# Router steps of the last attention stage on other units, and its score products in pairs

## The chip, the cores and the metric

The kernel runs on one core of a Trainium2 chip. The metric is the device time of one execution in microseconds. Instructions run on four engines: PE (TensorE), DVE (VectorE), ACT (ScalarE) and POOL (GpSimd). SP only issues DMAs, in its program order. Engines meet at semaphores, and each engine's instruction order is written out by hand.

## The reference

Two layers on x (2 batches, 512 rows, 1024 wide) and a context (2 x 1024 x 1024). The change lies where the second layer's grouped attention ends and its router begins:

```
q = (latents @ Wq.T)                    # 16 heads of 96, 4 key heads
scores = einsum('bkgqd,bksd->bkgqs', q, k) * scale      # 1536 keys
attn = softmax(scores)
out = einsum('bkgqs,bksd->bkgqd', attn, v)
x = x + tanh(g) * (out @ Wo.T)
# router and expert biases, 64 experts, the 8 best
logits = layernorm(x) @ router_weight.T + router_bias
scores = softmax(logits);  topk_w, topk_idx = top_k(scores, 8)
out = flat * w_sum + w_dense @ expert_bias
x = x + tanh(g) * out
```

Each fp32 operand of a product is split into a high and a low fp16 part, and three of the four partial products are summed.

## The kernel before, in words

Attention is done in 128 units m of 128 queries of one head against 1536 keys. They form 8 stages t of 16 units u (UPS = 16), a stage being one batch and one key head. The last stage begins at LAST = 112. Below, "unit 3" is the unit 3 of the last stage, "unit -1" the one before that stage; scores(3), exp(3) and so on are its steps. The tables of line 288 onwards count units in the same way.

In a unit, each engine does the following, in this order.

- **PE:** scores(u), six products over all 128 rows (the heads, L857) and three over 32 rows each (the rest, L835), into one of two sets of three PSUM banks. Then side work: router(i) for query tile i (24 small products, L599 with 64 columns), expert_turn(i) (L906), one half of an output product (L599 with 512 columns, nine products; wo_at gives the units 2, 3, 5, 6, 10, 11, 14 and 15) or expert_mix (L911, L912). Last weigh(u-3), 24 products that weigh the values (L880, L882), into bank 6.
- **DVE:** row_max(u) (L1659), for a router its logits (L1684) and choose_first (L1692 onwards), add_out (L1653) or add_mix (L1731), take_out(u-3) (L1673, L1675) and at last expert_stats(i) (L1398 onwards).
- **ACT:** take_o on every fourth unit, expert_weights (w_exp), exp(u) (L1325), the high cast hi(u) (L1054, region_b), expert_norm(i) (L1057 and L1054 on stage), expert_exp (L1301), expert_scale (L1057 on x_res).
- **POOL:** choose_rest(i), take_low_o, expert_low(i) (stage), the low part lo(u) (region_y, L1824), and for a tile with stats its deviations (rstd, nmr).
- **SP:** turn_o (L526), turn4(i) (L531, the transpose of tile i for the router), the transposes of hi(u) (L547) and lo(u) (L553). All DMAs of this stretch go through this one queue.

A tile's way to the router is expert_stats, deviations, expert_norm, expert_low, turn4, router; from there logits, expert_exp, choose_first, choose_rest, expert_turn, expert_weights, then two expert_mix and the store. Each step has a table from unit to tile. expert_stats(i) waits for the tile's last output product.

Four waits matter. scores(u) waits for exp(u-2), which frees its banks. weigh(u-3) waits for both transposes of unit u-3 and for take_out(u-4). router(i) and expert_turn(i) write bank 6, as weigh does: they wait for take_out(u-4), and the weigh behind a router waits until DVE has read its logits (lg_step), the one behind an expert_turn until ACT has made w_exp (wx_ok). expert_scale(i) and choose_rest(i) are waited for by add_mix and expert_turn.

Outside the last stage the rests of two units are paired: at an even unit u PE runs heads(u), rest(u), waits for exp(u-1), and runs rest(u+1) into the other banks; unit u+1 has then its heads alone. In the last stage, units are not paired.

After unit 15 comes a tail that is written out step by step: the last three weigh, the last output products, the routers of tiles 5, 6 and 7 and the last stores.

Of the kernel before, what the change touches and what calls it, by code (L numbers as in the profile page):

```python
# [54 lines left out]
def flamingo(nc, x_d, ctx_d, ctx_t_d, par_d, ident_d, wk_d, wv_d, wq_d, wo_d, wb_d, bb_d, ft_d,  # L55
             coef_d, mask_d, enc_d, rw_d, rb_d, eb_d, out_d):
    with ExitStack() as ctx:
# [227 lines left out]
        WQ_LOAD, WO_LOAD = {8: 0, 9: 1, 10: 2, 12: 3}, {3: 0, 4: 1, 5: 2, 6: 3}  # L285
        KV_LOAD = {0: 0, 1: 1, 2: 2, 7: 3, 13: 4}
        LAST = NU - UPS
        STATS4 = {-3: 0, -1: 1, 3: 2, 6: 3, 11: 4, 15: 5}
        NORM4 = {-2: 0, 0: 1, 4: 2, 7: 3, 12: 4}
        LOW4 = {-1: 0, 1: 1, 5: 2, 8: 3, 13: 4}  # L290
        ROUTE = {2: 0, 5: 1, 8: 2, 11: 3, 15: 4}
        CHOOSE = {3: 0, 6: 1, 9: 2, 12: 3}
        CHOOSE_REST = {4: 0, 7: 1, 10: 2, 13: 3}
        TURN_W = {6: 0, 9: 1, 12: 2, 14: 3}
        SCALE_X = {6: 0, 9: 1, 12: 2, 14: 3}
        MIX = {7: (0, 0), 8: (0, 1), 9: (1, 0), 12: (1, 1), 13: (2, 0)}
        STORE = {9: 0, 13: 1}

# [30 lines left out]
        def use(m, r):  # L329
            return 16 * (m // r + 1)  # L330
# [5 lines left out]
        def _(sp):  # L336
# [201 lines left out]
            for m in range(NU):  # L538
                t, u = m // UPS, m % UPS
                if o_at(m) is not None and m < NU - 1:  # L540
                    turn_o(o_at(m))
                if m - LAST in LOW4:
                    turn4(LOW4[m - LAST])
                if m >= PT:
# [50 lines left out]
        def _(pe):  # L595
# [243 lines left out]
            def scores(m):  # L839

                t, u = m // UPS, m % UPS
                b, qt, h = t % B, u // G, u % G
                if u == 0:
                    pe.wait_ge(k_ld[b], 5 * use(t, B))
                pairs = 2 <= m < LAST
                rest_behind = m % 2 == 0 or not pairs
                if m < G:
                    pe.wait_ge(q_set, min(m + 1, NJ))
                elif u == 0:
                    pe.wait_ge(q_free, 2 * NJ * (t + 1))  # L850
                    pe.wait_ge(q_dup, G * t)
                    pe.wait_ge(q_ld[b], 64 * ((t + t % 2) // 2))
                if m >= 2:
                    pe.wait_ge(e32_ok, m - 1)
                for n in range(2):
                    for sb_ in range(NSB):
                        ins = nc.tensor.matmul(bank(NSB * (m % 2) + sb_), q_head[:, b, h, n, qt * P:(qt + 1) * P],  # L857
                                               k_head[:, b, n, sb_ * 512:(sb_ + 1) * 512],
                                               start=rest_behind and n == 0, stop=not rest_behind and n == 1)
                if rest_behind:  # L860
                    ins = score_rest(m, False)
                    if pairs:
                        if m + 1 < G:
                            pe.wait_ge(q_set, min(m + 2, NJ))
                        pe.wait_ge(e32_ok, m)
                        score_rest(m + 1, True)
                ins.then_inc(sc_ready, 1)
# [59 lines left out]
            for m in range(NU):  # L927
# [4 lines left out]
                last = m - LAST  # L932
                if last in ROUTE:
                    pe.wait_ge(o_ok, m - LAG)
                    router(6, ROUTE[last])
                if last in TURN_W:
                    pe.wait_ge(o_ok, m - LAG)
                    expert_turn(6, TURN_W[last])
                w = wo_at(m)
# [16 lines left out]
                if m >= LAG:  # L956
                    if last in ROUTE:
                        pe.wait_ge(lg_step, ROUTE[last] + 1)
                    if last in TURN_W:
                        pe.wait_ge(wx_ok, TURN_W[last] + 1)  # L960
                    weigh(m - LAG)
# [90 lines left out]
        def _(act):  # L1052
# [261 lines left out]
            for m in range(NU):  # L1314
                t, u = m // UPS, m % UPS
                last = m - LAST
                if o_at(m) is not None and m < NU - 1:
                    take_o(o_at(m))
                if last in TURN_W:
                    expert_weights(6, TURN_W[last])  # L1320
                rows = ps[:, NSB * (m % 2):NSB * (m % 2 + 1), :].rearrange("p b n -> p (b n)")
# [23 lines left out]
                if t % 2 == 0 and u in WQ_SPLIT and t < TS - 2:  # L1345
                    act.wait_ge(q_ready, NJ * (t + 2))
                    wq_hi(CY_G + 1 + t, WQ_SPLIT[u])
                if last in NORM4:
                    expert_norm(NORM4[last])
                if last in ROUTE:  # L1350
                    expert_exp(ROUTE[last])
                if last in SCALE_X:
                    expert_scale(SCALE_X[last])

# [34 lines left out]
        def _(dve):  # L1389
# [359 lines left out]
            for m in range(NU):  # L1749
# [5 lines left out]
                if last in ROUTE:  # L1755
                    logits(6, ROUTE[last])
                if last in CHOOSE:
                    choose_first(CHOOSE[last])
                if m in V_AT:
# [9 lines left out]
                if m >= LAG:  # L1769
                    take_out(m - LAG)  # L1770
                if last in STATS4:
                    expert_stats(STATS4[last])

# [48 lines left out]
        def _(pool):  # L1822
# [126 lines left out]
            for m in range(NU):  # L1949
                t, u = m // UPS, m % UPS  # L1950
                if m - LAST in CHOOSE_REST:
                    choose_rest(CHOOSE_REST[m - LAST])
                if o_at(m) is not None and m < NU - 1:
                    take_low_o(o_at(m))
                if m - LAST in LOW4:
                    expert_low(LOW4[m - LAST])
                pool.wait_ge(exp_ok, m + 1)
# [5 lines left out]
                if t % 2 == 0 and u in WQ_SPLIT and t < TS - 2:  # L1963
                    split_wq(wq_n(t // 2 + 1) + WQ_SPLIT[u], WQ_SPLIT[u])
                if m - LAST in STATS4:
                    deviations(STATS4[m - LAST], LN4)
            expert_low(5)
# [71 lines left out]
```

## Time and profile before

| | |
|---|---|
| median of 3 runs | 1049.14 us (1048.36 to 1050.83) |
| the profiled execution's own time | 1048.36 us |
| its span, first to last instruction | 1046.6 us |
| busy share | PE 96%, DVE 61%, ACT 62%, POOL 62% |
| last stage, scores(0) to scores(15) | 916.82 to 1000.57 us |
| tail | from about 1004 us to the end |

Busy time of PE counts overlapping matmuls once; a row of the timeline that merges several instructions gives the start of the first and the time to the end of the last, and a matmul's end is modelled and overlaps the next one's start. So lengths of steps on PE are read from start to start. An idle gap stands behind a row in brackets, with what ended it.

### The profile page before, as it was taken

The page shows a single profiled execution, that of the slowest core. Times are in us where ns is not written, and L with a number is a line of the kernel's source. Part 1 is how long each engine was busy: PE and PEld are TensorE (multiplying, and loading weights), DVE is VectorE, ACT ScalarE, POOL GpSimd, SP SyncE. Part 2 cuts the span into 40 slices and gives each one's busy share as a digit, 9 for nine tenths or more (in the row PEclk, how much of TensorE's full clock was granted, in tenths as well). Part 3 has the DMA queues.
Part 4 walks back from the last instruction along what each step waited for, and adds up shares of the span by engine and source line. Part 5 has one row for each costly group of instructions (what it writes and reads, how often), then busy time and mean ns, then how long its engine had stood idle before and what let it go on. Part 6 is the DMA issues. An engine that isn't in the chain of part 4 may idle for free.

```text
span 1046.6 us, 18637 instructions
## 1 busy us (share of the span) xinstructions
PE 1006.5 (96%) x7262; PEld 556.5 (53%) x7262; DVE 642.6 (61%) x1109; ACT 652.1 (62%) x739; POOL 645.9 (62%) x348
## 2 busy tenths in 40 slices
PE   8999999999999989999999999999999999978977
PEld 4555444444554555555655555555555565545543
DVE  6889949754225556556656565565655665666557
ACT  5686534432123777667768767678766777778654
POOL 4477779333000678666668866668866667779661
PEclk9999999999999999999999999999999999999899
DMA  9986664852322999999999999999999999999985
GB/s 337 259 306 217 191 219 131 171 101 51 88 65 72 185 201 225 224 208 181 209 193 209 214 214 200 191 210 198 216 202 207 199 212 190 170 206 195 188 158 158
DMA packets 521179, 198.04 MB, mean 189 GB/s; under 512 B 485876, under 2 KB 503988, under 8 KB 521092
## 3 DMA queue, kind: packets, MB, share of 16 engines
q1 hardware_dynamic: 521092, 196.86, 90.8%
q8 instruction: 58, 0.95, 0.4%
q14 instruction: 29, 0.24, 0.1%
HBM read 59.24 MB, written 13.63 MB: 70 GB/s over the span
## 4 chain that ended last, share of the span: by engine, by line
PE 74%; DMA 9%; SPq 5%; DVE 4%; ACT 3%; POOL 3%; issue 2%; DVEq 0%; POOLq 0%; ACTq 0%
PE ps L599 33%; PE ps L857 11%; PE ps L815 10%; PE ps L880 9%; DMA region_o<-region_y 5%; PE ps L882 5%; PE ps L835 2%; POOL region_y L1824 2%; SPq L553 2%; SPq L547 2%; DMA region_c<-region_b 2%; ACT p L1325 1%; PE ps L621 1%; PE ps L740 1%; DVE p_max L1659 1%
## 5 line engine op out<-in xcount | busy, mean ns | idle before, releaser
L1824 POOL TENSOR_TENSOR region_y<-p,region_b 128x1536 f16<-128x1536 f32 x128 | 397.3, 3104 | 255.6 <-ACT region_b L1054 214.5
L1325 ACT ACTIVATE p<-ps,p_max 128x1536 f32<-128x1536 f32 x128 | 196.9, 1538 | 120.4 <-DVE p_max L1659 120.0
L1659 DVE TENSOR_REDUCE p_max<-ps 128x1 f32<-128x1536 f32 x128 | 224.7, 1756 | 74.7 <-PE ps L835 44.6
L1054 ACT ACTIVATE region_b<-p 128x1536 f16<-128x1536 f32 x128 | 189.7, 1482 | 65.0 <-DMA region_c<-region_b 59.2
L880 PE MATMUL ps<-region_q,region_c 128*128 128x192 f16 x1536 | 211.2, 248 | 15.3 <-DMA region_o<-region_y 13.5
L882 PE MATMUL ps<-region_q,region_o 128*128 128x96 f16 x1536 | 205.8, 208 | 0.0
L857 PE MATMUL ps<-region_q,region_c 128*128 128x512 f16 x768 | 189.4, 383 | 2.3 <-DMA region_q<-region_q 2.1
L880 PEld LDWEIGHTS ps<-region_q,region_c 128*128 128x128 f16 x1536 | 151.8, 99 | 40.7 <-issue 25.2
L882 PEld LDWEIGHTS ps<-region_q,region_o 128*128 128x128 f16 x1536 | 151.6, 99 | 11.0
L599 PE MATMUL ps<-region_w,region_q 128*128 128x512 f16 x576 | 136.7, 383 | 0.9 <-DVE region_q L1391 0.6
L815 PE MATMUL ps<-ln_t,region_w 128*128 128x512 f16 x576 | 131.8, 380 | 0.0
L1673 DVE TENSOR_SCALAR region_q<-ps,den_inv 128x96 f32<-128x96 f32 x128 | 40.6, 318 | 117.8 <-PE ps L882 115.5
L857 PEld LDWEIGHTS ps<-region_q,region_c 128*128 128x128 f16 x768 | 68.8, 99 | 65.1 <-issue 4.8
L815 PEld LDWEIGHTS ps<-ln_t,region_w 128*128 128x128 f16 x576 | 55.0, 98 | 71.9 <-issue 8.6
L599 PEld LDWEIGHTS ps<-region_w,region_q 128*128 128x128 f16 x576 | 54.2, 99 | 72.3 <-issue 11.9
L599 PE MATMUL ps<-region_c,ln_t 128*128 128x512 f16 x384 | 83.0, 379 | 0.4 <-DMA ln_t<-region_q 0.4
L1824 POOL TENSOR_TENSOR region_c<-stage,region_c 128x1024 f16<-128x1024 f32 (+1 forms) x25 | 53.3, 2149 | 17.5 <-ACT region_c L1054 17.5
L1824 POOL TENSOR_TENSOR rstd<-var_c,mhalf 128x1 f32<-128x1 f32 x32 | 25.3, 790 | 62.5 <-DVE var_c L1405 62.5
L599 PE MATMUL ps<-region_w,region_c 128*128 128x384 f16 x384 | 63.2, 326 | 0.0
L1054 ACT ACTIVATE region_o<-ps 128x384 f16<-128x384 f32 (+1 forms) x40 | 20.9, 536 | 67.7 <-PE ps L599 63.4
L599 PEld LDWEIGHTS ps<-region_c,ln_t 128*128 128x128 f16 x384 | 37.5, 98 | 46.0 <-issue 0.9
L1653 DVE SCALAR_TENSOR_TENSOR x_res<-ps,tg,x_res 128x512 f32<-128x512 f32 x64 | 47.8, 748 | 17.4 <-PE ps L599 14.4
(163 smaller groups left out, 1209.8 us busy)
## 6 DMA issues: line engine op xcount, KB each, us to landing
stage<-ctx_in SPq DMA_DIRECT2D x16, 512.0 KB, 4.8
stage<-ctx_t_in SPq DMA_DIRECT2D x15, 512.0 KB, 8.7
stage<-wq_in SPq DMA_DIRECT2D x16, 384.0 KB, 4.0
stage<-wo_in SPq DMA_DIRECT2D x16, 384.0 KB, 4.2
k_scratch<-region_o SPq DMA_DIRECT2D x12, 384.0 KB, 6.5
region_q<-k_scratch SPq DMA_DIRECT2D x8, 576.0 KB, 5.6
region_q<-v_scratch SPq DMA_DIRECT2D x8, 576.0 KB, 5.0
x_res<-x_in SPq DMA_DIRECT2D x8, 512.0 KB, 8.9
```

The lines of the kernel that those rows point to most:

```text
L547: sp.dma_start_transpose(pt_hi[:, m % PT, :, :], p_hi[:, m % 2, :]).then_inc(pt_hi_ld[m % PT], 16)
L599: ins = nc.tensor.matmul(out, a, b, start=first and n == 0, stop=last and n == len(pairs) - 1)
L815: ins = nc.tensor.matmul(by_tile(bank(at)), a, x, start=c == 0 and n == 0, stop=c == NC - 1 and n == 2)
L857: ins = nc.tensor.matmul(bank(NSB * (m % 2) + sb_), q_head[:, b, h, n, qt * P:(qt + 1) * P], k_head[:, b, n, sb_ * 512:(sb_ + 1) * 512], s ...
L880: nc.tensor.matmul(bank(6, VW), pt_hi[:, m % PT, i, :], v_head[:, b, i, :], start=i == 0, stop=False, skip_group_check=True)
L882: ins = nc.tensor.matmul(bank(6, HD), pt_lo[:, m % PT, i, :], v_head[:, b, i, 0:HD], start=False, stop=i == NS - 1, skip_group_check=True)
L1054: return nc.scalar.activation(out, in_, ACT.Copy)
L1325: nc.scalar.activation(p32[:, m % 2, :], rows, ACT.Exp, bias=p_max[:, m % 4:m % 4 + 1], accum_out=den[:, m % 4:m % 4 + 1]).then_inc(e32_ok, 1)
L1653: nc.vector.scalar_tensor_tensor(xh, bank(at), tg[:, 1:2], xh, ALU.mult, ALU.add).then_inc(wo_free, 1)
L1659: nc.vector.reduce_max(p_max[:, m % 4:m % 4 + 1], rows, axis=AX, negate=True).then_inc(max_ok, 1)
L1673: nc.vector.tensor_scalar(o_part[:, :], bank(6, VW)[:, HD:VW], d, None, ALU.mult).then_inc(part_ok, 1)
L1824: return nc.gpsimd.tensor_tensor(out, a, b, op)
```

## The change

Two things are changed. The tables that say on which unit each router step stands are altered: the steps of tile 0 up to turn4 stand one unit later, those of tile 1 up to turn4 one unit later and from the router on one earlier, those of tile 2 from the router on one or two earlier, and those of tile 3 from expert_stats to turn4 one later; MIX and STORE stay. And the pairing of the rests now holds in the last stage too (`m >= 2` without the upper end).

```diff
-        STATS4 = {-3: 0, -1: 1, 3: 2, 6: 3, 11: 4, 15: 5}
-        NORM4 = {-2: 0, 0: 1, 4: 2, 7: 3, 12: 4}
-        LOW4 = {-1: 0, 1: 1, 5: 2, 8: 3, 13: 4}
-        ROUTE = {2: 0, 5: 1, 8: 2, 11: 3, 15: 4}
-        CHOOSE = {3: 0, 6: 1, 9: 2, 12: 3}
-        CHOOSE_REST = {4: 0, 7: 1, 10: 2, 13: 3}
-        TURN_W = {6: 0, 9: 1, 12: 2, 14: 3}
-        SCALE_X = {6: 0, 9: 1, 12: 2, 14: 3}
+        STATS4 = {-2: 0, 0: 1, 3: 2, 7: 3, 11: 4, 15: 5}
+        NORM4 = {-1: 0, 1: 1, 4: 2, 8: 3, 12: 4}
+        LOW4 = {0: 0, 2: 1, 5: 2, 9: 3, 13: 4}
+        ROUTE = {2: 0, 4: 1, 7: 2, 11: 3, 15: 4}
+        CHOOSE = {3: 0, 5: 1, 8: 2, 12: 3}
+        CHOOSE_REST = {4: 0, 6: 1, 9: 2, 13: 3}
+        TURN_W = {5: 0, 8: 1, 10: 2, 14: 3}
+        SCALE_X = {5: 0, 8: 1, 10: 2, 14: 3}
         MIX = {7: (0, 0), 8: (0, 1), 9: (1, 0), 12: (1, 1), 13: (2, 0)}
         STORE = {9: 0, 13: 1}
...
-                pairs = 2 <= m < LAST
-                rest_behind = m % 2 == 0 or not pairs
+                rest_behind = m < 2 or m % 2 == 0
...
                     ins = score_rest(m, False)
-                    if pairs:
+                    if m >= 2:
                         if m + 1 < G:
                             pe.wait_ge(q_set, min(m + 2, NJ))
                         pe.wait_ge(e32_ok, m)
                         score_rest(m + 1, True)
```

On SP, around the first units of the last stage, the order before is this (L526 is turn_o, L531 turn4, L547 and L553 the transposes of hi and lo, from those of unit -1 on):

```order
394 L526 DMA_TRANSPOSE region_q<-region_q 128x6x128
395 L531 DMA_TRANSPOSE ln_t<-stage 128x16x128
396 L547 DMA_TRANSPOSE region_c<-region_b 128x12x128
397 L553 DMA_TRANSPOSE region_o<-region_y 128x12x128
398 L547 DMA_TRANSPOSE region_c<-region_b 128x12x128
399 L553 DMA_TRANSPOSE region_o<-region_y 128x12x128
400 L531 DMA_TRANSPOSE ln_t<-stage 128x16x128
```

And now, at the same place:

```order
394 L526 DMA_TRANSPOSE region_q<-region_q 128x6x128
395 L547 DMA_TRANSPOSE region_c<-region_b 128x12x128
396 L553 DMA_TRANSPOSE region_o<-region_y 128x12x128
397 L531 DMA_TRANSPOSE ln_t<-stage 128x16x128
398 L547 DMA_TRANSPOSE region_c<-region_b 128x12x128
399 L553 DMA_TRANSPOSE region_o<-region_y 128x12x128
400 L547 DMA_TRANSPOSE region_c<-region_b 128x12x128
```

turn4(0) has moved behind both transposes of unit -1, and turn4(1) behind those of unit 1.

On ACT, the rows of units 7 to 9 before, from exp(7) on (L1325 exp, L1054 on region_b the high cast, L1057 and L1054 on stage the norm, L1301 and w_exp router steps, L1057 on x_res the scale):

```order
502 L1325 ACTIVATE p,den<-ps,p_max 128x1536
503 L1054 ACTIVATE region_b<-p 128x1536
504 L1057 ACTIVATE stage<-x_res,nmr,rstd 128x1024
505 L1054 ACTIVATE stage<-stage 128x1024
506 L1325 ACTIVATE p,den<-ps,p_max 128x1536
507 L1054 ACTIVATE region_b<-p 128x1536
508 L1301 ACTIVATE logit,esum<-logit,nmx 128x64
509 L1054 ACTIVATE w_exp<-ps 128x128
510 L1325 ACTIVATE p,den<-ps,p_max 128x1536
511 L1054 ACTIVATE region_b<-p 128x1536
512 L1057 ACTIVATE x_res<-x_res,x_bias,x_scale 128x1024
```

And now (the file is one line shorter above this place, so each line number is one less):

```order
502 L1324 ACTIVATE p,den<-ps,p_max 128x1536
503 L1053 ACTIVATE region_b<-p 128x1536
504 L1300 ACTIVATE logit,esum<-logit,nmx 128x64
505 L1053 ACTIVATE w_exp<-ps 128x128
506 L1324 ACTIVATE p,den<-ps,p_max 128x1536
507 L1053 ACTIVATE region_b<-p 128x1536
508 L1056 ACTIVATE stage<-x_res,nmr,rstd 128x1024
509 L1053 ACTIVATE stage<-stage 128x1024
510 L1056 ACTIVATE x_res<-x_res,x_bias,x_scale 128x1024
511 L1324 ACTIVATE p,den<-ps,p_max 128x1536
512 L1053 ACTIVATE region_b<-p 128x1536
```

Norm 3 has moved from before exp(8) to before exp(9), and the scale of tile 1 from behind hi(9) to before exp(9).

On PE, unit 4 before (the end of weigh(0), scores(4), the start of weigh(1)):

```order
3075 L880 MATMUL ps<-region_q,region_c 128x192
3076 L882 MATMUL ps<-region_q,region_o 128x96
3077 L857 MATMUL ps<-region_q,region_c 128x512 x6
3078 L835 MATMUL ps<-region_q 128x512 x3
3079 L880 MATMUL ps<-region_q,region_c 128x192
```

And now:

```order
3073 L879 MATMUL ps<-region_q,region_c 128x192
3074 L881 MATMUL ps<-region_q,region_o 128x96
3075 L856 MATMUL ps<-region_q,region_c 128x512 x6
3076 L835 MATMUL ps<-region_q 128x512 x6
3077 L599 MATMUL ps<-region_s,ln_t 128x64 x24
3078 L879 MATMUL ps<-region_q,region_c 128x192
```

Six rest products stand here instead of three, and router(1) has come in between them and weigh(1).

## Rows read from the trace of the kernel before

**Rows 1.** Windows of the trace: us, busy time per engine, PEclk, DMA share, GB/s.

```profile
968.00:974.60 6.60, 6.42 (x32) 3.73 (x32) 1.97 (x9) 4.18 (x5) 5.11 (x2) 0.50 1.19 182
937.50:943.20 5.70, 3.16 (x35) 2.04 (x33) 3.99 (x9) 2.85 (x2) 2.23 (x3) 1.00 1.25 186
917.00:975.00 58.00, 49.42 (x455) 29.41 (x453) 37.66 (x88) 44.70 (x52) 49.97 (x39) 0.94 1.14 197
```

**Rows 2.** PE timeline, units -2 to 0: start, length, line, count, idle before.

```profile
906.70 1.46 PE L857 MATMUL ps<-region_q,region_c 128*128 128x512 f16 x6
...
908.62 2.12 PE L599 MATMUL ps<-region_w,region_q 128*128 128x512 f16 x9
910.58 0.25 PE L880 MATMUL ps<-region_q,region_c 128*128 128x192 f16 x1
...
912.08 1.46 PE L857 MATMUL ps<-region_q,region_c 128*128 128x512 f16 x6
913.37 2.10 PE L599 MATMUL ps<-region_w,region_q 128*128 128x512 f16 x9
...
916.82 1.46 PE L857 MATMUL ps<-region_q,region_c 128*128 128x512 f16 x6
...
918.53 0.26 PE L880 MATMUL ps<-region_q,region_c 128*128 128x192 f16 x1
```

**Rows 3.** DVE timeline, units -1, 11 and 12.

```profile
913.57 1.76 DVE L1659 TENSOR_REDUCE p_max<-ps 128x1 f32<-128x1536 f32 x1 [0.54 <-PE ps L857]
...
985.25 1.28 DVE L1398 BATCH_NORM_STATS2 bn<-x_res 128x6 f32<-128x512 f32 x2
...
987.04 1.75 DVE L1659 TENSOR_REDUCE p_max<-ps 128x1 f32<-128x1536 f32 x1
```

**Rows 4.** POOL timeline, units -1 and 0: low part of tile 0, then lo(-1).

```profile
918.40 2.13 POOL L1824 TENSOR_TENSOR stage<-stage 128x1024 f16<-128x1024 f32 x1
920.48 3.11 POOL L1824 TENSOR_TENSOR region_y<-p,region_b 128x1536 f16<-128x1536 f32 x1
```

**Rows 5.** The line of turn4 (L531), units 0 to 13: from issue to landing.

```profile
DMA to landing us min/median/max: 4.8/5.5/5.9
```

**Rows 6.** PE timeline, units 2 to 15.

```profile
923.79 1.46 PE L857 MATMUL ps<-region_q,region_c 128*128 128x512 f16 x6
...
927.26 0.86 PE L599 MATMUL ps<-region_s,ln_t 128*128 128x64 f16 x24 [1.69 <-DMA ln_t<-stage]
...
941.68 0.24 PE L880 MATMUL ps<-region_q,region_c 128*128 128x192 f16 x1 [2.54 <-DMA region_o<-region_y]
...
963.80 1.46 PE L857 MATMUL ps<-region_q,region_c 128*128 128x512 f16 x6
...
968.18 0.58 PE L911 MATMUL ps<-region_s,w_exp 128*128 128x512 f16 x1 [2.44 <-ACT w_exp L1054]
...
974.71 0.39 PE L835 MATMUL ps<-region_q 32*128 32x512 f16 x3
...
978.49 1.46 PE L857 MATMUL ps<-region_q,region_c 128*128 128x512 f16 x6
...
984.36 1.46 PE L857 MATMUL ps<-region_q,region_c 128*128 128x512 f16 x6
...
1004.58 0.88 PE L599 MATMUL ps<-region_s,ln_t 128*128 128x64 f16 x24 [2.23 <-DMA ln_t<-stage]
```

**Rows 7.** ACT timeline, units 12 and 13.

```profile
990.55 1.48 ACT L1054 ACTIVATE region_b<-p 128x1536 f16<-128x1536 f32 x1
991.94 1.23 ACT L1057 ACTIVATE stage<-x_res,nmr,rstd 128x1024 f32<-128x1024 f32 x1
...
994.16 1.23 ACT L1057 ACTIVATE x_res<-x_res,x_bias,x_scale 128x1024 f32<-128x1024 f32 x1
995.29 1.52 ACT L1325 ACTIVATE p<-ps,p_max 128x1536 f32<-128x1536 f32 x1
...
996.99 1.48 ACT L1054 ACTIVATE region_b<-p 128x1536 f16<-128x1536 f32 x1
```

## The prediction, made before the changed kernel ran

> **What bounds the kernel now.** I first looked at the busy shares: PE is 96% busy over the span, so outside the last stage only work taken off PE counts, and the change does nothing there. Then the windows of the last stage [rows 1]: in the 58 us from 917 to 975 PE is busy for 49.4 (85%), POOL for 50.0, and the DMA engines are loaded above one (1.14) at 197 GB/s. No engine is full; the stage is bound by a net of waits. Then the PE timeline for where it stands still [rows 6]: 1.69 us at router(0), until the transpose of tile 0 has landed; 2.54 at weigh(1), until lo(1) has landed; 2.44 at expert_mix(1,0), until w_exp is made, since expert_turn(1) stands right before it in unit 9; 2.23 at router(4). After the third the clock was half: granted 0.50, the 1.2 GHz level, from 968 to 974.6 [rows 1], so the heads of unit 10, which take 1.39 us otherwise, ended only at 974.71 [rows 6].
>
> **Lengths, from start to start [rows 2].** Heads alone 1.29 (912.08 to 913.37). Unpaired scores 1.71 (916.82 to 918.53). Paired scores with both rests 1.92 (906.70 to 908.62). Nine output products 1.96, weigh 1.50. A router is 0.70, a mix 0.65, a turn 0.1. On DVE, from the end of weigh(8) at 984.36 through take_out and expert_stats to row_max(12) at 987.04 are 2.68 us, of which the stats 1.79 [rows 3, 6]; row_max takes 1.67, and from its start to the high cast of its unit are 3.5 (987.04 to 990.55) [rows 3, 7]. On ACT exp takes 1.7, the high cast 1.4, expert_norm 2.2 (991.94 to 994.16), the scale 1.13 [rows 7]. On POOL the low part of a tile takes 2.1 and lo(u) 3.1 [rows 4].
>
> **Pairing alone.** Two unpaired scores are 3.42, a pair is 1.92 + 1.29 = 3.21: 0.21 us per pair, eight pairs, 1.7 us of PE work. It is only gained where PE doesn't wait anyway. It also adds a wait: at an even unit exp(u-1) must be done before the rest of u+1, one unit earlier than now, and side work and weigh are queued behind it.
>
> **The walk through the stage.** I put the new order on these lengths, starting from the profiled times.
>
> Unit 2, router(0). The stats of tile 0 now stand before row_max(-1), which began at 913.57 after 0.54 of idling [rows 3]; with 1.79 of stats it begins at 914.8. hi(-1) is then at 918.3 and done at 919.8, lo(-1) done at 922.9; the low part of tile 0, which stood before it [rows 4], comes behind it and ends at 925.0. With 5.5 us to landing [rows 5] router(0) starts at 930.6, against 927.26 [rows 6]. (The new wait for exp(1), about 926.8, lies inside this.) It was followed by 0.64 of waiting for lo(-1), which goes. Router, output and weigh end at 934.8.
>
> Unit 4. The late unit 2 could hide in the 2.54 us before weigh(1), for lo(1) need no longer be late. But router(1) has come into this unit, and no output product lies between it and weigh(1), as it does in unit 5. Weigh(1) waits until DVE has read the logits, and DVE has take_out(0) and the stats of tile 2 before it: weigh(0) ends at 934.8 + 1.29 + 1.96 + 1.50 = 939.55; plus 2.68, plus row_max 1.67 and the logits 0.4, 944.3. Before: 941.68 [rows 6]. +2.6.
>
> Units 5 to 8. In unit 5 expert_turn(0) makes weigh(2) wait for w_exp, which ACT reaches after hi(4) (942.2 + 3.5 = 945.7), norm 2 and the logits' exp: 950.0, a wait of 0.85. Unit 6 is 1.92 + 1.96 + 1.50 = 5.4: 956.9. Unit 7 now has router(2); its logits are read behind row_max(7), and weigh(4) is 960.5 to 962.0. Unit 8 is 1.92 + 0.1 + 0.65 + 1.50: scores(9) at 966.2, against 963.80. +2.4.
>
> Unit 9. Here the gain is. Expert_turn(1) is gone from it, and expert_mix(1,0) waits only for add_mix(0,1): row_max(8) at 962.0 + 2.68 = 964.7, plus 1.67, choose_first 0.7 and add_mix 0.8 is 967.9. The heads of unit 10 end at 967.9 + 0.65 + 1.50 + 1.39 = 971.4, against 974.71 at half clock: -3.3.
>
> Unit 10. The pair waits for exp(9). Before exp(9) ACT now has norm 3 and the scale of tile 1: hi(8) at 964.7 + 3.5 = 968.2, plus 1.4, 2.2, 1.13 and 1.7 is 974.7. PE stands still for 3.0 us. Rest, turn, output, weigh: scores(11) at 978.5, against 978.49. All is given back.
>
> Unit 11, router(3). Low 3 now follows choose_rest(2) on POOL behind lo(8), with turn4(3) behind. The same row of steps is in the trace before, in units 12 to 15: from hi(12) at 990.55 to router(4) at 1004.58, 14.0 us [rows 6, 7]. From hi(8), 968.2 + 14.0 = 982.2, where PE arrives at 979.8. Scores(12) is at 982.2 + 0.70 + 1.96 + 1.50 = 986.4, against 984.36: +2.0. With the shortest landing of rows 5, 4.8, it is +1.3.
>
> From there to the end the order of the steps that decide is the old one: take_out(8), stats 4, row_max(12), hi(12), lo(12), choose_rest(3), low 4, turn4(4), router(4), then the tail. The earlier scale of tile 2 brings exp(13) 1.1 us forward (995.29 to 994.2 in the old times), but POOL, which takes lo(13) after low 4, is later anyway. So +2.0 goes through.
>
> Clock. The half-clock stretch of unit 9 is already out of this sum. A new one is not in it: in unit 2 PE stands still for about 4.3 us in two pieces, longer than the 2.44 that was followed by one. The stretch behind that cost 3.0 us on PE (0.4 in the mix, 1.4 in weigh, 1.2 in the heads); from below, nothing, as after the 2.54 at 941.68, where the clock stayed at 1.00 [rows 1]. Even less than nothing is possible, since the one after router(4) in the tail may stay away, some 1.7. I take 0.7, low between the ends, because waits behind it absorb a part.
>
> Sum: +2.0 + 0.7 = +2.7. Against the profiled execution's own 1048.36 that makes 1051.1; that one is 0.8 below the median, so with the median of 1049.14 the forecast is 1051.8.
>
> A page of the Trainium skill bears on this ("TensorE: Matmul & The Clock Gate", section "HAM oscillation"): bursts of matmuls with DMA waits between them are throttled again and again. By that rule the idle of units 2, 10 and 11 would each bring a slow stretch, three times 3.0, and the sum would be about +11. Of the waits of over 2 us in rows 6 this trace agrees for two and disagrees for one, so I keep the smaller term.
>
> **Rivals.**
>
> Faster: the waits don't come as late as walked. It is decided in unit 10: if exp(9) is done when PE arrives at 971.7 and tile 3 has landed when router(3) is reached, 3.0 and 2.0 go, and with a part of the pairs' 1.7 the sum is -3: 1046. For it speaks that the collision of unit 9 with its half clock, 5.4 us together, surely goes. Against it speaks the order on ACT, where 3.3 us of new work stand before exp(9).
>
> No change: the DMA queue sets the pace. The load was 1.14 at 197 GB/s, and the same transposes have to go through it between units 0 and 11. Then the order of the engines matters little, and waits on PE only change places: -0.7 to +1.2, 1049. Against it: PE and POOL fell behind the queue in unit 9 because of the half clock.
>
> Another page of the Trainium skill ("DMA: Bandwidth & Descriptors", section "Latency and other measured facts") gives DMA transposes 261 GB/s. The queue would then have a quarter to spare and this rival would fall; our trace doesn't show such a rate.
>
> Much slower: a full half-clock stretch of 6.6 us in unit 2 or 10, where nothing absorbs it: +2.0 + 3.0, 1054, and with two of them 1056.
>
> **How the numbers follow.** A measurement of this kernel can't tell less than 0.2% (2.1 us) from no change. Forecast, slower by 1.3 to 4: 0.45. Much slower: 0.12. No change by the queue: 0.23. Faster: 0.20. A third of the forecast's chance lies below +2.1 (no clock term), so: faster 0.19, same 0.35, slower 0.46. The range is 1046.3 to 1054.5; its lower end takes in most of the faster rival. The likeliest case's own range is 1050.4 to 1053.2.
>
> **What would show it.** Right: in the profile after, router(0) waits 3 us or more for the transpose; weigh(1) waits for the logits, not for a DMA; the gap before expert_mix(1,0) falls under 0.6; in unit 10 PE waits about 3 us between the rests of two units, for ACT; router(3) waits about 2 us; a pair in the last stage is 3.2 us where it doesn't wait. Wrong: scores(12) less than 67 us after scores(0) (67.5 before, 69.5 forecast), or a tail that isn't the old one from router(4) on, or the waits in units 10 and 11 missing.

## The result: slower by 0.35 to 0.5%, more than forecast

| | before | after |
|---|---|---|
| median, first comparison (5 executions each) | 1049.35 us | 1055.9 us, ratio 1.0053 [1.0040, 1.0067] |
| median, second comparison (35 and 12 executions) | 1049.88 us | 1053.38 us, ratio 1.0035 [1.0015, 1.0054] |
| profiled execution, its own time and span | 1048.36, 1046.6 us | 1052.36, 1050.6 us |
| scores(0) to scores(12) | 67.5 us | 72.1 us |
| scores(12) to the end | 62.2 us | 60.0 us |

One of the five executions of after took 5673 us and doesn't count in the ratio; the median of the 21 others on record is 1054.8 us.

The forecast was 1051.8 with a range up to 1054.5. The direction was right; the first comparison ended above the range by either median, the second inside it, at 1053.4. Of the 4.0 us between the two profiled executions, 1.6 lie before scores(0) (918.45 against 916.82), and in four profiles of before that start lies between 916.8 and 925.0. So the stages are compared from scores(0) on.

The page of after has PE busy for 1006.3 us, against 1006.5, in a span 4 us longer: in the sums the whole difference is idle time, and where it arose only the timeline tells. The rows of the PE timeline of after that answer to [rows 6] (start, length, line, count, idle before; lines from 846 on are one less than before):

```profile
918.45 1.46 PE L856 MATMUL ps<-region_q,region_c 128*128 128x512 f16 x6
...
928.25 0.39 PE L835 MATMUL ps<-region_q 32*128 32x512 f16 x3 [1.19 <-ACT p L1324]
932.41 1.44 PE L599 MATMUL ps<-region_s,ln_t 128*128 128x64 f16 x24 [3.77 <-DMA ln_t<-stage]
933.66 3.63 PE L599 MATMUL ps<-region_w,region_q 128*128 128x512 f16 x9
...
938.62 1.46 PE L856 MATMUL ps<-region_q,region_c 128*128 128x512 f16 x6
...
948.04 0.26 PE L879 MATMUL ps<-region_q,region_c 128*128 128x192 f16 x1 [1.88 <-DVE logit L1683]
...
953.80 0.26 PE L879 MATMUL ps<-region_q,region_c 128*128 128x192 f16 x1 [0.74 <-ACT w_exp L1053]
...
969.84 1.46 PE L856 MATMUL ps<-region_q,region_c 128*128 128x512 f16 x6
971.82 0.38 PE L910 MATMUL ps<-region_s,w_exp 128*128 128x512 f16 x1 [0.52 <-DVE x_res L1730]
...
973.96 1.46 PE L856 MATMUL ps<-region_q,region_c 128*128 128x512 f16 x6
975.35 0.39 PE L835 MATMUL ps<-region_q 32*128 32x512 f16 x3
978.31 0.61 PE L835 MATMUL ps<-region_q 32*128 32x512 f16 x3 [2.56 <-ACT p L1324]
978.85 0.29 PE L905 MATMUL ps<-ident_h,w_tok 128*128 128x128 f16 x1
978.93 4.05 PE L599 MATMUL ps<-region_w,region_q 128*128 128x512 f16 x9
...
985.12 1.46 PE L856 MATMUL ps<-region_q,region_c 128*128 128x512 f16 x6
...
990.56 1.46 PE L856 MATMUL ps<-region_q,region_c 128*128 128x512 f16 x6
```

Router(0) waits 3.77 for the transpose, weigh(1) 1.88 for its logits, weigh(2) 0.74 for w_exp, the gap ahead of expert_mix(1,0) has shrunk from 2.44 to 0.52, and PE waits 2.56 between the two rests of unit 10. All of that was forecast. (Weigh(2) waits because the new tables put expert_turn and expert_scale of tile 0 one unit earlier too, in unit 5, which the list of the change leaves out; the diff has it.) A pair that doesn't wait takes 3.23 us (units 6 and 7), as forecast. The wait of about 2 us at router(3) is missing: router(3) starts right behind the heads of unit 11. That was named as a sign of being wrong, and so was a tail that isn't the old one, which came as well. Also not forecast is what stands behind the waits of units 2 and 10: the router takes 1.44 instead of 0.86, and nine output products 3.63 and 4.05 instead of 2.12. The windows over both places (columns as in [rows 1]):

```profile
930.30:937.10 6.80, 4.69 (x33) 2.54 (x34) 0.45 (x2) 5.63 (x7) 6.33 (x5) 0.53 1.14 209
978.00:984.80 6.80, 6.49 (x32) 3.51 (x33) 2.58 (x4) 6.04 (x8) 6.80 (x4) 0.52 0.94 158
```

The granted clock is about 0.5, the 1.2 GHz level, for 6.8 us each time. The profile of before that the prediction used had one such stretch (unit 9) and a shorter one behind router(4).

### The profile page after: what moved, and what is told of

Its sections match the earlier page's. It is cut to its first block, busy times and chain, and to the rows that moved or that the text cites. A ratio compares the mean times of both kernels' runs of the same rounds, so it can differ in the third digit from the quotient of the medians.

```text
span 1050.6 us, 18637 instructions
## 1 busy us (share of the span) xinstructions
PE 1006.3 (96%) x7262; PEld 556.4 (53%) x7262; DVE 641.3 (61%) x1109; ACT 651.9 (62%) x739; POOL 645.1 (61%) x348
## 4 chain that ended last, share of the span: by engine, by line
PE 68%; DMA 11%; SPq 6%; DVE 4%; POOL 4%; ACT 3%; issue 2%; DVEq 0%; POOLq 0%; ACTq 0%
PE ps L599 33%; PE ps L856 10%; PE ps L815 9%; PE ps L879 8%; DMA region_o<-region_y 6%; PE ps L881 4%; SPq L553 3%; SPq L547 2%; POOL region_y L1823 2%; PE ps L835 2%; DMA region_c<-region_b 2%; DVE p_max L1658 1%; ACT p L1324 1%; PE ps L621 1%; DMA ln_t<-stage 1%
## 5 line engine op out<-in xcount | busy, mean ns | idle before, releaser
L1658 DVE TENSOR_REDUCE p_max<-ps 128x1 f32<-128x1536 f32 x128 | 224.6, 1755 | 73.2 <-PE ps L835 39.9
L1823 POOL TENSOR_TENSOR region_c<-stage,region_c 128x1024 f16<-128x1024 f32 (+1 forms) x25 | 53.4, 2156 | 17.8 <-ACT region_c L1053 17.7
```

Of the source, the lines that this page charges most:

```text
L1658: nc.vector.reduce_max(p_max[:, m % 4:m % 4 + 1], rows, axis=AX, negate=True).then_inc(max_ok, 1)
L1823: return nc.gpsimd.tensor_tensor(out, a, b, op)
```

## The experiments

Sixteen runs. All ratios but the first of after are against before on the same chip (11 or 12 executions against 34 or 35). "Fillers" are products whose result nobody reads. "Stage" is the time from scores(0) of the last stage to the end of the span in the profiled execution; "half clock" is the sum of the stretches at the 1.2 GHz level from scores(0) up to and behind router(4). The stretch in the last microseconds, which every kernel has, is left out.

| kernel | ratio [interval] | stage, us | scores(12), us after scores(0) | half clock, us |
|---|---|---|---|---|
| before, four profiles | 1 | 129.8, 127.9, 128.2, 128.7 | 67.5, 66.9, 65.9, 66.5 | 10.2, 6.8, 3.4, 6.8 |
| after, three profiles | 1.0053 [1.0040, 1.0067], 1.0035 [1.0015, 1.0054] | 132.2, 132.0, 132.0 | 72.1, 71.0, 71.9 | 13.6, 13.6, 13.6 |
| pairs alone | 0.9995 [0.9978, 1.0011] | 127.7 | 66.7 | 10.2 |
| tables alone | 1.0031 [1.0013, 1.0048] | 133.1 | 72.2 | 13.6 |
| after, tiles 0 and 1 early | 1.0018 [1.0000, 1.0035] | 129.4 | 68.6 | 6.8 |
| after, tiles 0, 1, 3 early | 1.0009 [0.9995, 1.0023] | 128.1 | 67.1 | 6.8 |
| after, 16 fillers in the wait of unit 2 | 0.9998 [0.9979, 1.0017] | 127.2 | 68.0 | 0 |
| after, 8 fillers there | 1.0003 [0.9986, 1.0020] | 129.2 | 69.9 | 6.8 |
| after, 16 fillers behind that wait | 1.0052 [1.0035, 1.0068] | 132.5 | 73.2 | 3.4 |
| before, 11 fillers in unit 9 | 0.9984 [0.9969, 0.9998] | 126.8 | 66.4 | 0 |
| pairs, fillers in units 2, 9, 14 | 0.9993 [0.9976, 1.0009] | 128.3 | 66.3 | 6.8 |
| early tiles 0, 1, 3, 11 fillers in unit 2 | 0.9978 [0.9961, 0.9994] | 127.2 | 67.8 | 6.8 |
| another set of tables | 1.0024 [1.0009, 1.0039] | 131.3 | 70.4 | 13.6 |

The theories: the walk (the tables make waits, as in the prediction); the pairing carries the loss; the clock (the half-clock stretches behind the waits carry it); the DMA queue sets the pace.

**Pairs alone** (before with the pairing in the last stage):

```
-                pairs = 2 <= m < LAST
+                pairs = 2 <= m
```

> The tables of before, with the pairing of the rests also in the last stage. Theory W (the loss comes from router steps put where they are waited for; the pairing is nearly free): ratio to before 0.999 to 1.001, a pair takes 3.2 us where it doesn't wait; the wait for exp(1) in unit 2 takes the place of the wait for the transpose of tile 0. Rival P (the pairing's early wait for exp is the loss): at least 2 us slower than before, 1.002 or more, with waits of PE for ACT between two rests that sum to over 4 us.

1050.13 us, ratio 0.9995. The added wait for exp(1) is there, 2.86 us in unit 2, and router(0) no longer waits behind it. The waits for ACT between two rests sum to 6.3 us (2.86, 0.91 and 2.56), more than the 4 of the rival, but they take the place of other waits. The pairing is free within the measurement, and the rival that it carries the loss falls.

**Tables alone** (after, with `pairs = 2 <= m < LAST` as before):

> The tables of after, with unpaired rests in the last stage. Theory W: as slow as after or up to 1 us slower, 1.005 to 1.007; the 3 us wait for exp(9) in unit 10 then stands elsewhere, as a wait of expert_turn(2) for take_out(6) (which waits for the scale of tile 1), and router(3) still waits 1.5 us or more. Rival P: 1.002 or less.

1053.37 us, ratio 1.0031. Router(0) waits in one piece, and router and output products are slow again:

```profile
935.91 1.44 PE L599 MATMUL ps<-region_s,ln_t 128*128 128x64 f16 x24 [5.16 <-DMA ln_t<-stage]
937.16 3.10 PE L599 MATMUL ps<-region_w,region_q 128*128 128x512 f16 x9
```

The tables carry the loss. The ratio is below the 1.005 to 1.007 that was expected. Expert_turn(2) waits 2.49 us for DVE in unit 10, as expected, but router(3) doesn't wait, which wasn't.

**16 fillers in the wait of unit 2.** After, and ahead of router(0), 16 fillers:

```
                     pe.wait_ge(o_ok, m - LAG)
+                    if last == 2:
+                        for _ in range(16):
+                            nc.tensor.matmul(bank(6), ones_h[:, :], eb_hi[:, 0:512], start=True, stop=True)
                     router(6, ROUTE[last])
```

> The kernel after, with 16 products of ones times expert biases (512 columns each, 3.4 us at full clock) into bank 6 in unit 2, before PE waits for the transpose of tile 0. Router(0) overwrites them. Theory C (half of what the walk missed, some 2 to 3 us, is the half-clock stretch behind the 3.8 us wait of unit 2): no half clock in units 2 to 4, scores(12) 1.5 to 3 us earlier after scores(0) than the 72.1 of after, ratio to before 1.002 to 1.004. Rival (the clock's part is absorbed by the logits wait in unit 4): unchanged, 1.005.

1050.28 us, ratio 0.9998. The PE timeline of this kernel, and its windows over the same two places:

```profile
929.90 3.63 PE L936 MATMUL ps<-region_s,ones_h 128*128 128x512 f16 x16
933.36 0.86 PE L599 MATMUL ps<-region_s,ln_t 128*128 128x64 f16 x24
934.06 2.11 PE L599 MATMUL ps<-region_w,region_q 128*128 128x512 f16 x9
...
937.50 1.46 PE L856 MATMUL ps<-region_q,region_c 128*128 128x512 f16 x6
...
972.84 1.46 PE L856 MATMUL ps<-region_q,region_c 128*128 128x512 f16 x6
...
977.18 0.39 PE L835 MATMUL ps<-region_q 32*128 32x512 f16 x3 [2.57 <-ACT p L1327]
977.57 2.11 PE L599 MATMUL ps<-region_w,region_q 128*128 128x512 f16 x9
981.02 1.46 PE L856 MATMUL ps<-region_q,region_c 128*128 128x512 f16 x6
983.58 0.86 PE L599 MATMUL ps<-region_s,ln_t 128*128 128x64 f16 x24 [1.11 <-DMA ln_t<-stage]
...
987.72 1.46 PE L856 MATMUL ps<-region_q,region_c 128*128 128x512 f16 x6
```

```profile
929.90:936.70 6.80, 6.80 (x63) 3.85 (x61) 1.24 (x5) 5.95 (x6) 6.72 (x5) 1.00 1.13 227
976.80:983.60 6.80, 5.31 (x44) 3.09 (x45) 4.38 (x7) 6.53 (x9) 6.80 (x4) 1.00 0.95 158
```

The fillers begin and end inside the wait. Router(0) starts 13.6 us after scores(0) (14.0 in after), so nothing came earlier; but from there to scores(3) are 4.14 us instead of 6.21, since the clock stayed at 1.00. In unit 10 PE waits the same 2.57 us as in after, and this time no half clock follows. The waits are those of after, or nearly; the slow stretches are gone, and with them 4.8 us of the stage (132.0 to 127.2) and 0.37 to 0.55% of the time, more than the theory had said. The clock theory stands.

What the fillers themselves do ends at scores(10): there the kernel is 2.4 us ahead of after. That no half clock followed in unit 10 can't be put down to them. The next run has fillers in unit 2 and half clock in unit 10, the one behind it has half clock in unit 2 and none in unit 10, both with the same wait of 2.56 us.

**Half as many fillers** (`range(8)`):

> The changed kernel with 8 products of no use ahead of router(0), half as many as before. They take 1.7 us of its wait, and 1.9 to 2.1 of idling stay. Theory (it is the length of the idling that counts): with an idle of 2.0, near the 2.44 and 2.56 that were followed by half clock in some executions and not in others, a stretch of 3.4 us or none in unit 2; scores(3) 17.7 to 19.2 us after scores(0), ratio 1.000 to 1.002. Rival (any gap there brings the whole loss): scores(3) at 20.2 to 20.5, ratio 1.0035 or more.

1051.53 us, ratio 1.0003. Its PE timeline in unit 2:

```profile
930.80 1.90 PE L936 MATMUL ps<-region_s,ones_h 128*128 128x512 f16 x8
934.43 0.87 PE L599 MATMUL ps<-region_s,ln_t 128*128 128x64 f16 x24 [1.74 <-DMA ln_t<-stage]
935.14 2.11 PE L599 MATMUL ps<-region_w,region_q 128*128 128x512 f16 x9
```

No half clock follows the 1.74 us that are left, and scores(3) is at 17.9 us. A stretch of 6.8 us came in unit 10 all the same:

```profile
978.00:984.80 6.80, 6.53 (x32) 3.55 (x33) 2.54 (x4) 6.00 (x8) 6.80 (x4) 0.52 0.95 158
```

Scores(12) is late by 1.9 against 16 fillers; the medians don't tell the two apart.

**The same 16 products behind router(0)**, ahead of the output product, into bank 7:

```
                     side_free(m)
+                    if last == 2:
+                        for _ in range(16):
+                            nc.tensor.matmul(bank(7), ones_h[:, :], eb_hi[:, 0:512], start=True, stop=True)
                     out_product(7, w)
```

> The changed kernel with 16 products of no use in unit 2 again, but behind router(0) and ahead of the output product, where PE has work, and into bank 7. It leaves the wait for the transpose as it is. Theory (what the earlier filler run gained came from PE being busy in the wait): router(0) waits 3.6 to 3.8 as in the changed kernel, half clock follows, and the products come on top of it, 3.4 us at full and up to 6.8 at half clock: scores(3) 24 to 26 us after scores(0), ratio 1.006 to 1.010. Rival (the products help wherever they stand in the unit, by their number): ratio 1.000 to 1.003, no half clock.

1056.54 us, ratio 1.0052, just under the expected 1.006 to 1.010, and scores(3) at 23.0 us, under the expected 24 to 26. The wait is whole, half clock follows, and the fillers themselves run slow:

```profile
934.30 1.44 PE L599 MATMUL ps<-region_s,ln_t 128*128 128x64 f16 x24 [3.80 <-DMA ln_t<-stage]
935.56 4.45 PE L953 MATMUL ps<-region_s,ones_h 128*128 128x512 f16 x16
```

So it is not the products that help but their standing in the wait. They cost less than their own 3.4 us, since the stretch was 3.4 us here instead of 6.8 and none followed in unit 10, behind the same wait of 2.56 us:

```profile
982.60:989.40 6.80, 5.34 (x45) 3.13 (x46) 4.38 (x7) 6.52 (x9) 6.80 (x4) 1.00 0.96 158
```

**Tiles 0 and 1 early** (after with stats, norm and low part of tiles 0 and 1 on before's units):

```
-        STATS4 = {-2: 0, 0: 1, 3: 2, 7: 3, 11: 4, 15: 5}
+        STATS4 = {-3: 0, -1: 1, 3: 2, 7: 3, 11: 4, 15: 5}
```

(NORM4 and LOW4 likewise.)

> The kernel after, but stats, norm, low part and transpose of tiles 0 and 1 back on the units of before (-3/-1, -2/0, -1/1). Theory W: router(0) waits at most 1 us for the transpose (behind the wait for exp(1)); the wait for logits in unit 4 and the waits of units 10 and 11 stay; with the half-clock stretch of unit 2 gone, 2.5 to 4 us faster than after: ratio to before 1.002 to 1.003. Rival Q (the DMA queue sets the pace, waits only change places): as slow as after, 1.005.

1051.76 us, ratio 1.0018. The PE timeline of its unit 2:

```profile
931.69 0.39 PE L835 MATMUL ps<-region_q 32*128 32x512 f16 x3 [2.75 <-ACT p L1324]
932.01 0.87 PE L599 MATMUL ps<-region_s,ln_t 128*128 128x64 f16 x24
932.72 2.11 PE L599 MATMUL ps<-region_w,region_q 128*128 128x512 f16 x9
```

PE waits for exp(1) and no longer for the transpose, and all lengths behind it are those of full clock. That may be this execution's: behind nearly the same wait the pairs alone (2.86) and the next run (2.94) have 3.4 us of half clock in their profiles. A new wait of 2.63 us, for POOL, stands at expert_turn(0) in unit 5. The same transposes go through the same queue, yet the stage is 2.6 us shorter. The interval leaves out the 1.0053 of after, and just takes in the 1.0035. The stronger evidence against the rival of the DMA queue is the run with 16 fillers, which has the transposes of after in their order and none of the loss.

**Tiles 0, 1 and 3 early**:

> The changed kernel with the steps of tiles 0, 1 and 3 up to the low part back on the units they had before; what stays of the change is the pairing, router(1) and router(2) one unit earlier and the expert steps behind them. Theory (walk plus clock): no wait for the transpose in unit 2, weigh(1) waits 1.9 for its logits, router(3) doesn't wait; without the clock 0 to +0.5 us against before, with one stretch of 3.4 us at half clock 1.7 more: 1050 to 1052. Rival (the earlier routers 1 and 2 carry the loss): ratio 1.003 or more, 1053 or more, with scores(12) 70 us or more after scores(0).

1050.97 us, ratio 1.0009, as the theory had it. The earlier routers 1 and 2 and their expert steps, with the pairs, cost about nothing that the medians show.

**Before, 11 fillers in unit 9**, ahead of expert_mix(1,0), into bank 7:

> The kernel before with 11 products of no use into bank 7 in unit 9, ahead of expert_mix(1,0), where PE stands still for 2.44 us. Theory (the clock there costs what PE loses, 3.0 us, and nothing behind it gives that back): the stretch of 6.6 us at half clock is gone, scores(12) 64.5 to 65.5 us after scores(0) (67.5 before), 1046 to 1047, ratio 0.997. Rival (a wait behind it absorbs it, as my prediction took for a part of it): the stretch is gone, but PE waits 2 to 3 us more in units 10 or 11 for ACT or the transpose of tile 3; ratio 0.9995 to 1.0005.

1048.36 us, ratio 0.9984: faster than before, by less than the theory said. Scores(12) is at 66.4, not 64.5 to 65.5: the output product of unit 10 now waits 1.28 for add_mix,

```profile
970.06 2.54 PE L957 MATMUL ps<-region_s,ones_h 128*128 128x512 f16 x11
972.58 0.39 PE L911 MATMUL ps<-region_s,w_exp 128*128 128x512 f16 x1
...
977.79 1.46 PE L599 MATMUL ps<-region_w,region_q 128*128 128x512 f16 x6 [1.28 <-DVE x_res L1734]
```

so about 1.9 of the 3.0 us that the stretch cost PE in my profile was given back behind it. Against the further profiles of before (65.9 to 66.9) scores(12) isn't earlier at all; its stage is the shortest because no half clock fell behind unit 14 or router(4) either, far behind the fillers. Both were half right.

**Pairs with fillers in units 2, 9 and 14**:

> The kernel before with the pairing in the last stage, and 11 products of no use where PE then stands still: between the two rests in units 2 and 14 (2.9 and 2.6 us) and ahead of expert_mix(1,0) in unit 9 (2.8 us). Theory (clock): the three stretches of 3.4 us at half clock that the paired kernel had are gone, each worth 1.0 to 1.7: 1046 to 1047.5, ratio 0.996 to 0.998. Rival (waits behind them absorb it, and pairs bring nothing): ratio 0.999 to 1.001.

1049.98 us, ratio 0.9993, a miss. The stretches in units 2 and 9 are gone, but one of 3.4 us came in unit 4, behind a wait of 1.96 us of weigh(1) for its transpose, and the one of unit 14 stayed. The fillers in unit 14 were put behind a wait for bank 6 to be read, so they came after the idling and not in it, and ran at half clock:

```profile
997.71 4.23 PE L868 MATMUL ps<-region_s,ones_h 128*128 128x512 f16 x11 [2.41 <-DVE region_c L1682]
```

**Early tiles with 11 fillers in unit 2**, between the two rests, where PE stood still for 2.9 us (it is the run with tiles 0, 1 and 3 early, and this):

```
+                        if m == LAST + 2:
+                            pe.wait_ge(o_ok, m - LAG)
+                            for _ in range(11):
+                                nc.tensor.matmul(bank(6), ones_h[:, :], eb_hi[:, 0:512], start=True, stop=True)
                         pe.wait_ge(e32_ok, m)
                         score_rest(m + 1, True)
```

> The changed kernel with tiles 0, 1 and 3 early as in the run before, and 11 products of no use between the two rests of unit 2, where PE stood still for 2.9 us. Theory: the stretch of 3.4 us at half clock there goes, 1.0 to 1.5 us with it; scores(12) 65.5 to 66 us after scores(0) (67.1 without them), 1048 to 1049.5, ratio 0.998 to 0.9995. Rival (waits behind take it back, as in the paired kernel with three fills): ratio 1.0005 or more.

1048.14 us, ratio 0.9978 [0.9961, 0.9994]: the lowest ratio of all, ahead of both kernels, but not told apart from that of before with 11 fillers (0.9984). Unit 2 has no half clock, and router(0) starts 11.8 us after scores(0). Scores(12), at 67.8 in the profile, missed the expected 65.5 to 66, with a stretch of 3.4 us in unit 7 behind a wait of 1.90. That profile is of the slowest of the 12 executions (1052.92 us), so the gain is seen in the medians alone.

**Another set of tables**, unpaired, found by carrying the walk of the prediction through many tables:

```
-        CHOOSE = {3: 0, 6: 1, 9: 2, 12: 3}
-        TURN_W = {6: 0, 9: 1, 12: 2, 14: 3}
+        CHOOSE = {3: 0, 7: 1, 10: 2, 12: 3}
+        TURN_W = {7: 0, 9: 1, 12: 2, 14: 3}
```

(LOW4, CHOOSE_REST and SCALE_X changed with them.)

> The kernel before, unpaired, with other tables: the steps of tile 0 after its router one unit later (choose_rest stays, expert_turn in unit 7), those of tile 1 up to the low part one unit later and choose_first one later, choose_first of tile 2 in unit 10. Expert_turn stands in a unit of its own ahead of each mix then. By the walk through the waits it should save about 2 us up to router(4) where no half clock follows: 1047 to 1048, ratio 0.997 to 0.999. Rival (what the tables win in waits the clock takes back, or the walk is blind for it): ratio 1.000 or more.

1053.92 us, ratio 1.0024, a miss. Its profiled stage has stretches of 3.4, 6.8 and 3.4 us, and scores(12) at 70.4. A walk without the clock chose badly; how much of the loss is the clock's was not tested here.

**After once more**, beside these:

> The changed kernel itself once more, beside the others of this batch. Theory (the stretches at half clock are worth about 5 us of it, as the run with filler products in unit 2 gave): ratio to before 1.004 to 1.0065, two stretches of 6.8 us in the last stage or as much in smaller ones, and scores(12) 71 to 73 us after scores(0). Rival (the gain of the filler run was a matter of its chip and hour): ratio 1.000 to 1.002 here.

1053.38 us, ratio 1.0035, just below what was expected, with scores(12) at 71.0.

**More profiles of before (three) and of after (one)**, one execution each. What was asked is in the expectation of the first; those of the other two profiles of before ask the same.

> The kernel before once more, for its profile. Theory (the profiled execution that I worked from had an unusually dear last stage): from scores(0) to the end 127 to 128.5 us, against 129.8 there, with at most 6.8 us at half clock in all between scores(0) and router(4). Rival (it was typical): 129.3 to 130.3, with a stretch of 6.8 us in unit 9 and 3.4 behind router(4).

> The changed kernel, a third profile. Theory: 131.5 to 133.5 us from scores(0) to the end, with half clock behind the waits of units 2 and 10. Rival (its stretches come and go as those of before do): between 127.2, as with filler products in unit 2 and no stretch, and 133.5, most often near 130.

Before: stages of 127.9, 128.2 and 128.7 us, against 129.8 in the profile that I had worked from; two of the three lie where the theory had them. After: 132.0, as the theory had it. In all four profiles of before, PE waits the same 2.44 us ahead of expert_mix(1,0). The windows behind that wait, of the first, second and third further profile:

```profile
973.30:976.70 3.40, 3.40 (x17) 1.75 (x14) 0.95 (x2) 2.41 (x2) 2.93 (x2) 0.52 1.29 149
```

```profile
970.00:976.80 6.80, 5.39 (x42) 3.00 (x43) 3.14 (x10) 4.20 (x5) 6.29 (x4) 1.00 1.20 185
```

```profile
978.10:981.50 3.40, 3.40 (x20) 1.75 (x16) 0.79 (x2) 2.58 (x2) 2.94 (x2) 0.52 1.30 147
```

So the half clock that the prediction's gain of unit 9 rested on (6.6 us, 3.0 of it lost on PE) is 6.8, 3.4, 0 and 3.4 us from one execution to the next.

## Why the prediction was too low, step by step

Times are us after scores(0), at 916.8 in [rows 2]. The run with 16 fillers is after without half clock, one profile.

| step | forecast | after | after, 16 fillers |
|---|---|---|---|
| router(0) | 13.8 | 14.0 | 13.6 |
| scores(3) | 18.0 | 20.2 | 17.7 |
| weigh(1), waits for the logits | 27.5 | 29.6 | 27.1 |
| weigh(2) waits for w_exp | 0.85 | 0.74 | 0.72 |
| scores(9) | 49.4 | 51.4 | 49.0 |
| unit 10 waits for exp(9) | 3.0 | 2.56 | 2.57 |
| scores(11) | 61.7 | 66.7 | 61.2 |
| router(3) waits | 2.4 | 0 | 1.11 |
| scores(12) | 69.5 | 72.1 | 68.0 |
| scores(12) to the end | 62.2 | 60.0 | 59.3 |

**The walk was right up to unit 10.** Units 2 to 10, without the clock, agree within 0.5 us. The added waits up to there stand where they were put, with the releasers that were named, and unit 10 gave back nearly all that unit 9 had gained: scores(11) is 0.5 us earlier than before. The pairing brings about nothing, as forecast. In unit 11 the walk was too long, see below.

**The step that failed is the clock term: "I take 0.7, low between the ends, because waits behind it absorb a part."** The stretches of after cost 4.8 us in the profiles, and 3.9 to 5.8 in the medians (0.9998 against 1.0035 and 1.0053, each against before on its own chip). The term also allowed for the stretch behind router(4) to stay away. It did, and the tail of before is 1.8 us longer with it (62.2 against 60.4 in the run with fillers). Like for like, then, the term is 3.0 where 0.7 stood, in a range from -1.7 to +3.0. I had counted one stretch, partly absorbed. In fact stretches stood behind the waits of units 2 and 10 in all three profiles of after (6.8 and 6.8; 6.8, 3.4 and a further 3.4 behind unit 14; 6.8 and 6.8). Nothing absorbed the first: scores(3) is 2.5 us later than with fillers and scores(10) 2.4. The second cost 1.6 to 3.0 between scores(10) and scores(11) (9.8 and 11.2 us against 8.2), and 1.3 of it came back in unit 11, where router(3) then didn't have to wait. The rest, 0.8, lies in the tail, where after has no half clock in that profile. The first part is shown by the fillers and by the same products behind the wait. The second compares executions with and without a stretch in unit 10, which no experiment controlled.

The rule of the Trainium skill ("TensorE: Matmul & The Clock Gate", section "HAM oscillation") was weighed in the prediction and set aside. It named the right mechanism: bursts with waits between them were throttled in every profile of after. The count of two for and one against it was short by a wait: the 2.50 us of unit 14 in before, which the rows left out, were not followed by half clock either. Its sum of +11 was too much, since of the three places two were slowed, and together they cost 4.8 us, not three times 3.0. The chance of 0.12 that I gave to a full stretch with nothing to absorb it was too low: two such stretches are what came. (Two small slips stand in these numbers. Two stretches, +2.0 and twice 3.0, make 1057.1 on the median and not 1056, and the four chances add up to 0.20 faster, 0.38 same and 0.42 slower, not 0.19, 0.35 and 0.46.)

**A second error lay in the base.** I worked from one profiled execution of before and took its half clock for a property of the kernel. Its stage was 129.8 us; three others have 127.9 to 128.7, mean 128.3. Of these 1.5 us, 1.1 lie before scores(12) (67.5 against a mean of 66.4) and stand behind unit 9, and 0.4 in the tail. In unit 4 that execution was late too: weigh(1) started 24.9 us after scores(0) there, behind the 2.54 of [rows 6], and at 24.1, 23.5 and 23.8 in the others, with waits of 1.29 to 1.40. But that cost nothing: scores(9) is at 47.0 there and at 47.1 to 47.7 in the others, which wait 1.5 to 1.6 us in unit 5 for the transpose of turn_o instead. Against that one profile, the stage of after is +2.3 us, and the forecast was +2.7. That this is close is luck: the clock is 2.3 above its term, the walk 1.6 and the tail 1.1 below. Against the other three it is +3.8, near what the medians show (+3.5 and +5.5).

**Two errors on the other side hid part of it.** The transpose of tile 3 came earlier than walked: from hi(8) to router(3) are 12.8 us, not 14.0, and without half clock scores(12) is at 68.0 and not 69.5. The ACT timeline of the run with 16 fillers (to be read with its row of router(3), 983.58) and the landing of that transpose in it:

```profile
970.78 1.48 ACT L1056 ACTIVATE region_b<-p 128x1536 f16<-128x1536 f32 x1
```

```profile
ln_t<-stage SPq DMA_TRANSPOSE x1, 4.4
```

The landing took 4.4 us, under the 4.8 that was the shortest of [rows 5]. And "the tail is the old one" was wrong: without half clock it takes 60.4 in before (with fillers) and 59.3 in after (with fillers), 1.1 less. Two other versions of after without half clock in the tail have 59.3 and 59.4; the two profiles of after itself that have none there, 60.0 and 60.1. The tail holds the last four units, where the pairs come in too, and I had counted nothing for them there. That it is the pairs isn't shown. Where a stretch of 3.4 us falls behind unit 14, before has 61.0, the pairs alone 61.0 and after 61.0, no difference at all.

The account, all from profiled stages, mostly one each: walk and pairs +0.4 (127.2 against 126.8, both with fillers and no half clock); clock in after +4.8; clock in before, which has to be taken off, -1.5 on average of the three further profiles and -2.9 in the one that I used. Together +3.7, or +2.3. The two comparisons of medians, +5.5 (with the median of the 21) and +3.5 us, lie 2 us apart, but their intervals, [1.0040, 1.0067] and [1.0015, 1.0054], overlap, so nothing shows that they differ. What stays open is how much of the second stretch each execution of after has: three were profiled.

## What to carry to other kernels

Where an engine order is walked through, the waits can come out well, and the clock is a term of its own: a wait of TensorE of some microseconds can have a price on what runs behind it, here 2.4 us for a stretch of 6.8 in unit 2. If the wait can't be removed, products without use, into a free bank and inside the wait, are cheap; they must stand ahead of whatever PE waits for, in a bank that is free by then. And before half clock is booked as a gain, look at more than one profile: the same wait may have none in the next execution.

## What the runs showed of the hardware that was not expected

The same 2.44 us of idling, at the same place of the same kernel, was followed by 6.8, 3.4, 0 and 3.4 us at the 1.2 GHz level. In after the 2.56 us of unit 10 were followed by 6.8, 3.4 and 6.8 us; in four versions of it with the same wait by 3.4 (tiles 0 and 1 early), 6.8 (8 fillers in unit 2), 0 (16 fillers) and 0 (16 fillers behind the wait of unit 2). So whether unit 2 ran at half clock doesn't settle it. Waits of 1.90 and 1.96 us were followed by 3.4 in two runs, one of 1.74 and one of 2.75 by none. A longer wait didn't bring a longer stretch: 5.16 us in the run with the tables alone brought 3.4, 3.80 with the fillers behind brought 3.4, and 3.6 to 3.8 in after 6.8.

Products without use need not cost time: with 11 of them (2.5 us in their row) before was faster by 0.16% [0.02, 0.31].
